# Rows gathered under the last strips, late rows added by extra gathers and accumulating scatters

## The reference

```python
h = jnp.maximum(_layernorm(x, axis=-1), 0.0)
x = x + _L0_gnn_ref(h, ...)     # tanh(h, t) W1 W2 + adj @ (h B^T) - rowsum(adj) * (h B^T)
h = jnp.maximum(_layernorm(x, axis=-1), 0.0)
x = x + _L1_gnn_ref(h, adj, ...)
# inside the second layer
feats = (X @ W).reshape(-1, H, D)
scores = jax.nn.leaky_relu(a_self.T[:, :, None] + a_neigh.T[:, None, :], negative_slope=0.2)
scores = scores + (-10000000000.0 * (1.0 - A))[None, :, :]
attn = jax.nn.softmax(scores, axis=-1)
out = relu(einsum('hij,jhd->ihd', attn, feats) + bias)
```

## Time and profile before

| | us |
|---|---|
| median of 3 runs | 891.37 (890.23 to 891.55) |
| the profiled execution | 890.93 |
| its span on the core | 889.1 |

### The profile page before, as it was taken

How to read it: one execution, slowest core, us unless ns; L and a number is a source line. 1 busy time by engine, 2 the same in 40 slices (tenths; PEclk the granted TensorE clock), 3 DMA queues, 4 the chain that set the end, 5 groups by cost and what they waited for, 6 DMA issues and landing times.

```text
span 889.1 us, 13351 instructions
## 1 busy us (share of the span) xinstructions
PE 765.8 (86%) x5222; PEld 275.1 (31%) x5222; DVE 728.0 (82%) x958; ACT 130.0 (15%) x212; POOL 173.9 (20%) x160
## 2 busy tenths in 40 slices
PE   3898999999999999999999999999999999940000
PEld 1323343333333333434343434333333333320000
DVE  5889889999898989898989898989989898943111
ACT  2424011111102020202020202011111102020000
POOL 1000303030201102030303030303020110217775
PEclk9999999999999999999999999999999999975555
DMA  9796898989898989898989989898989898501221
GB/s 372 280 429 255 342 389 327 393 330 389 336 387 364 382 342 386 332 391 335 386 337 383 371 348 392 328 392 328 392 328 392 359 384 352 221 17 40 52 58 43
DMA packets 37261, 281.48 MB, mean 317 GB/s; under 512 B 14336, under 2 KB 18560, under 8 KB 20736
## 3 DMA queue, kind: packets, MB, share of 16 engines
q1 hardware_dynamic: 24704, 275.02, 76.8%
q0 software_dynamic: 4096, 4.20, 2.0%
q10 hardware_dynamic: 8448, 2.10, 1.0%
HBM read 277.10 MB, written 4.19 MB: 316 GB/s over the span
## 4 chain that ended last, share of the span: by engine, by line
PE 83%; POOL 7%; SPq 4%; issue 3%; DMA 1%; DVE 1%; ACT 1%; POOLq 0%; ACTq 0%; DVEq 0%
PE acc L719 48%; PE row_sums L727 25%; POOL gathered L359 7%; SPq L256 4%; PE ps_hid L734 2%; PE ps_feat L776 1%; PE ps_xb L755 1%; PE ps_acc L748 1%; PE ps_turn L762 1%; DMA ring<-in_adj_t 1%; PE ps_acc L753 1%; PE ps_acc L751 1%; PE ps_turn L769 1%; POOL cand L350 0%; DMA gathered<-feats_dram,best 0%
## 5 line engine op out<-in xcount | busy, mean ns | idle before, releaser
L719 PE MATMUL acc<-ring,x_pb 128*64 128x512 f32 x2048 | 448.3, 594 | 0.0
L727 PE MATMUL row_sums<-ring,ones_cols 128*32 128x512 f32 x2048 | 234.3, 602 | 18.6 <-DMA ring<-in_adj_t 18.6
L505 DVE TENSOR_TENSOR max_lo<-max_lo,ring 128x2048 f32<-128x2048 f32 x96 | 219.7, 2288 | 37.5 <-DMA ring<-in_adj_t 36.7
L719 PEld LDWEIGHTS acc<-ring,x_pb 128*64 128x64 f32 x2048 | 143.8, 137 | 282.7 <-issue 280.9
L506 DVE TENSOR_TENSOR max_hi<-max_hi,ring 128x2048 f32<-128x2048 f32 x96 | 219.7, 2288 | 0.0
L350 POOL DMA_INDIRECT cand<-in_adj,cls_row x64 | 77.1, 1205 | 650.5 <-DVE cls_row L535 635.8
L727 PEld LDWEIGHTS row_sums<-ring,ones_cols 128*32 128x32 f32 x2048 | 61.6, 111 | 164.0 <-issue 159.2
L359 POOL DMA_INDIRECT gathered<-feats_dram,best x64 | 63.3, 989 | 19.5 <-issue 19.5
L643 DVE TENSOR_TENSOR gathered<-gathered,bias_row 128x512 f32<-128x512 f32 x8 | 5.6, 695 | 68.1 <-DMA gathered<-feats_dram,best 68.1
L427 ACT COPY feats<-ps_feat 128x320 f32 (+1 forms) x16 | 6.8, 426 | 216.4 <-PE ps_feat L776 216.4
L512 DVE TENSOR_TENSOR max_lo<-max_lo,max_hi 128x2048 f32<-128x2048 f32 x16 | 36.7, 2293 | 2.0
(11 more groups left out here) (95 smaller groups left out, 415.6 us busy)
## 6 DMA issues: line engine op xcount, KB each, us to landing
ring<-in_adj_t SPq DMA_DIRECT2D x128, 2048.0 KB, 9.3
x_tq<-in_x SPq DMA_DIRECT2D x1, 2048.0 KB, 31.0
feats_dram<-feats ACTq DMA_DIRECT2D x16, 128.0 KB, 2.6
out<-gathered SPq DMA_DIRECT2D x8, 256.0 KB, 2.2
x_pb<-in_x SPq DMA_DIRECT2D x1, 1536.0 KB, 7.8
cand<-in_adj,cls_row POOLq DMA_INDIRECT x64
gathered<-feats_dram,best POOLq DMA_INDIRECT x64, 2.4
x_pb<-in_x SPq DMA_DIRECT2D x1, 512.0 KB, 4.6
```

Source lines behind the costliest of these rows:

```text
L505: dve.tensor_tensor(max_lo[:, :], max_lo[:, :], lo, ALU.max).then_inc(lo_done, 1)
L719: last = pe.matmul(acc[0][at:at + D, :], x_pb[:, c * CB + b, :], slot(c)[:, b * W:(b + 1) * W], start=(c == 0 and b < 2), stop=(c == NC - ...
L727: last = pe.matmul(row_sums[at:at + QUAD, :], ones_cols[:, :], slot(c)[:, b * W:(b + 1) * W], start=(c == 0 and b < 4), stop=(c == NC - 1 ...
```

## The change

GpSimd keeps a DRAM table `agg_dram` in place of `feats_dram`: it holds relu(feats + bias). In the round of a strip GpSimd waits for ScalarE's copy of the features, adds the bias and takes the maximum with 0 in two instructions, issues the store from its own queue and waits until it has landed (`store_agg`). ScalarE's store is gone. Before the strips, the rows of strips 11 to 15 of the table are set to zero by five stores.

The 64 gathers are split into windows. Where the rows of `known` strips are in the table, tiles of strips s0 to s1 are gathered: 4, 16, 16, 16 and 8 tiles in the rounds 11 to 15, and 4 tiles at the end. A tile whose best row is not yet in the table reads zeros for it. VectorE lists up to 8 such late rows in each partition by their keys (`max` gives the 8 largest); GpSimd gathers those rows again in 8 indirect gathers at the end, and adds them to the output by 8 accumulating indirect scatters, four before and four after the gathers of the last two tiles. Partitions with fewer late rows spend the other slots on rows of the last strip, which is stored after all scatters. More than 8 late rows in a partition clear `good`, and so lead to the general path.

The last strip's table rows are computed by VectorE from PSUM (`agg_last`) and stored by SP. On VectorE the classes of the last strip are searched before its residual. x1 is added to the gathered rows in three instructions (52, 8 and 4 tiles) in place of sixteen; the output goes out in four stores, the first of which only fills the last strip. At the start, the first chunk is issued between the two pieces of x, x_tq comes after chunk 7, and the 17 weight loads move from SP's queue to GpSimd's.

```diff
+WINDOWS = ((11, 0, 1), (12, 1, 5), (13, 5, 9), (14, 9, 13), (15, 13, 15))
+EARLY = 13 * TB
+LATE = 15 * TB
...
+            load_x(0, 0, 2 * CB)
+            sp.dma_start(slot(0), adj_t[0]).then_inc(chunk_in[0], 16)
+            load_x(1, 2 * CB, NB)
+            for n in range(1, RING):
+                sp.dma_start(slot(n), adj_t[n]).then_inc(chunk_in[n], 16)
...
             for c in range(RING, NC):
                 load(0, c)
+            sp.dma_start(x_tq[:, :, :].rearrange("q (s k) d -> q s (k d)", k=TB), x_by_q).then_inc(x_tq_in, 16)
...
+            sp.dma_start(out_by_q[:, S - 1, :], x_pb[:, 0:TB, :].rearrange("q k d -> q (k d)")).then_inc(stored, 16)
+
+            sp.wait_ge(got[len(WINDOWS) - 1], 16 * (LATE - EARLY))
+            sp.wait_ge(agg_last_ready, 2)
+            sp.dma_start(agg_by_q[:, S - 1, :], agg_last[:, :, :].rearrange("q k d -> q (k d)")).then_inc(agg_last_stored, 16)
...
+            store(0, 0, EARLY)
+            store(1, EARLY, LATE)
+            sp.wait_ge(late_out, 16 * SLOTS)
+            store(2, LATE, NB)
...
+            for z in range(WINDOWS[0][0], S):
+                pool.dma_start(agg_by_q[:, z, :], agg[:, :]).then_inc(zero_stored, 16)
...
+            def store_agg(s):
+
+                pool.wait_ge(feat_done, s + 1)
+                a = feats_v[:, bass.ds(s * TB, TB), 0:D]
+                pool.tensor_tensor(agg[:, :].rearrange("q (k d) -> q k d", d=D), a,
+                                   bias_row[:, :].unsqueeze(1).to_broadcast([P, TB, D]), ALU.add).then_inc(agg_chain, 1)
+                pool.wait_ge(agg_chain, s * 2 + 1)
+                pool.sem_inc(pool_past, 1)
+                pool.tensor_scalar(agg[:, :], agg[:, :], 0.0, None, ALU.max).then_inc(agg_chain, 1)
+                pool.wait_ge(agg_chain, s * 2 + 2)
+                pool.dma_start(agg_by_q[:, bass.ds(s, 1), :].rearrange("q a f -> q (a f)"), agg[:, :]).then_inc(agg_stored, 16)
+                pool.wait_ge(agg_stored, s * 16 + 16)
...
+            for w, (known, s0, s1) in enumerate(WINDOWS):
+                add_b2(known)
+                if w:
+                    pool.wait_ge(got[w - 1], 16 * TB * (WINDOWS[w - 1][2] - WINDOWS[w - 1][1]))
+                store_agg(known - 1)
+                pool.wait_ge(best_done, s1)
+                if known < S - 1:
+                    gather(w, s0 * TB, s0 * TB + TB)
+                    fetch_candidates(known)
+                    gather(w, s0 * TB + TB, s1 * TB)
+                else:
+                    gather(w, s0 * TB, s1 * TB)
+                    fetch_candidates(known)
+
+
+            pool.wait_ge(agg_last_stored, 16)
+            pool.wait_ge(late_ready, 2)
+            for k in range(SLOTS):
+                pool.indirect_dma_start(
+                    out=late_agg[:, k, :], out_offset=None, in_=agg_dram,
+                    in_offset=bass.IndirectOffsetOnAxis(ap=late_from[:, k:k + 1], axis=0),
+                ).then_inc(late_in, 16)
+            pool.wait_ge(best_done, S)
+            gather(len(WINDOWS), LATE, LATE + 2)
+            pool.wait_ge(late_in, 16 * SLOTS)
+            pool.wait_ge(stored, 16 * 3)
+
+            def scatter(k):
+                pool.indirect_dma_start(
+                    out=out, out_offset=bass.IndirectOffsetOnAxis(ap=late_row[:, k:k + 1], axis=0),
+                    in_=late_agg[:, k, :], in_offset=None, compute_op=ALU.add,
+                ).then_inc(late_out, 16)
+
+            for k in range(TB):
+                scatter(k)
+            gather(len(WINDOWS), LATE + 2, NB)
+
+            pool.wait_ge(late_out, 16 * TB)
+            for k in range(TB, SLOTS):
+                scatter(k)
...
+            for known, s0, s1 in WINDOWS:
+                dve.tensor_scalar(is_late[:, s0 * TB:s1 * TB], best[:, s0 * TB:s1 * TB], float(known * W), None, ALU.is_ge)\
+                    .then_inc(late_chain, 1)
+            dve.tensor_tensor(late_key[:, :], best[:, 0:LATE], late_span[:, :], ALU.add).then_inc(late_chain, 1)
...
+            for w in range(len(WINDOWS) - 1):
+                dve.wait_ge(got[w], 16 * TB * (WINDOWS[w][2] - WINDOWS[w][1]))
+            add_x1(0, EARLY)
             search_candidates(S - 1)
+            dve.wait_ge(got[len(WINDOWS) - 1], 16 * (LATE - EARLY))
+            add_x1(EARLY, LATE)
```

More of the change, by code:

```diff
@@ L61, in sem @@
             return ctx.enter_context(nc.semaphore(name))
-        feats_dram = nc.dram_tensor("feats_dram", (N, D), F32, kind="Internal").ap()
+        agg_dram = nc.dram_tensor("agg_dram", (N, D), F32, kind="Internal").ap()
         neigh_dram = nc.dram_tensor("neigh_dram", (HEADS, N), F32, kind="Internal").ap()
@@ L185, in build @@
         best_done = sem("best_done")
-        got = [sem(f"got{g}") for g in range(QG)]
+        got = [sem(f"got{w}") for w in range(len(WINDOWS) + 1)]
+        late_chain = sem("late_chain")
+        late_ready = sem("late_ready")
+        late_in = sem("late_in")
+        late_out = sem("late_out")
         end_chain = sem("end_chain")
@@ L241, in _, with load_x @@
         def _(sp):
-            for k, (b0, b1_) in enumerate(((0, 2 * CB), (2 * CB, NB))):
+            def load_x(k, b0, b1_):
                 sp.dma_start(x_pb[:, b0:b1_, :], x_by_p[:, b0:b1_, :]).then_inc(x_in[k], 16)
[L244 to L261, removed]
+            load_x(0, 0, 2 * CB)
[3 more added lines that the diff above has]
+                sp.dma_start(slot(n), adj_t[n]).then_inc(chunk_in[n], 16)
             def load(s, c):
@@ L353, in _, with gather @@
                     ).then_inc(cand_in, 16)
[L354 to L358, removed]
-                pool.indirect_dma_start(
-                    out=gathered[:, t, :], out_offset=None, in_=feats_dram,
-                    in_offset=bass.IndirectOffsetOnAxis(ap=best[:, t:t + 1], axis=0),
-                ).then_inc(got[t // OG], 16)
+            def gather(w, t0, t1):
+                for t in range(t0, t1):
+                    pool.indirect_dma_start(
+                        out=gathered[:, t, :], out_offset=None, in_=agg_dram,
+                        in_offset=bass.IndirectOffsetOnAxis(ap=best[:, t:t + 1], axis=0),
+                    ).then_inc(got[w], 16)
@@ new lines, in round_ @@
+            def round_(s):
+                add_b2(s)
+                store_agg(s - 1)
+                fetch_candidates(s)
+            add_b2(0)
+            fetch_candidates(0)
+            n0 = WINDOWS[0][0]
+            with pool.Fori(1, n0) as s:
+                round_(s)
+            for w, (known, s0, s1) in enumerate(WINDOWS):
[11 more added lines that the diff above has]
+                    fetch_candidates(known)
@@ new lines, in _ @@
+            dve.scalar_tensor_tensor(late_at[:, :], late_s[:, :], -float(P), late_base[:, :], ALU.mult, ALU.add)\
+                .then_inc(late_chain, 1)
+            dve.wait_ge(late_chain, n + 7)
+            dve.tensor_tensor(late_row[:, :], late_at[:, :], late_k[:, :], ALU.subtract).then_inc(late_ready, 1)
+            dve.wait_ge(feat_ready, S)
+            dve.tensor_tensor(agg_last[:, :, :], ps_feat[:, :, 0:D], bias_row[:, :].unsqueeze(1).to_broadcast([P, TB, D]),
+                              ALU.add).then_inc(agg_last_ready, 1)
@@ new lines, in _, with add_x1 @@
+            dve.wait_ge(agg_last_ready, 1)
+            dve.tensor_scalar(agg_last[:, :, :], agg_last[:, :, :], 0.0, None, ALU.max).then_inc(agg_last_ready, 1)
+            def add_x1(t0, t1):
+                dve.tensor_tensor(gathered[:, t0:t1, :], gathered[:, t0:t1, :], x_tq[:, t0:t1, :], ALU.add)\
+                    .then_inc(out_done, 1)
+            for w in range(len(WINDOWS) - 1):
+                dve.wait_ge(got[w], 16 * TB * (WINDOWS[w][2] - WINDOWS[w][1]))
+            add_x1(0, EARLY)
@@ L637, in _ @@
             dve.tensor_scalar(flag[:, :], ps_hid[0:1, 0:1], P - 0.5, None, ALU.is_lt).then_inc(flag_done, 1)
[L640 to L649, removed]
+            dve.wait_ge(got[len(WINDOWS)], 16 * (NB - LATE))
+            add_x1(LATE, NB)
             dve.wait_ge(flag_done, 1)
```

97 lines of the change are left out of this document (76 added, 21 removed).

## The result

The changed kernel takes 858.74 us (median of 4 runs, 855.85 to 861.41) where the kernel before takes 891.46: a ratio of 0.9635, with a 95% interval of 0.9603 to 0.9668. It is faster, by 32.7 and not by the 61.7 of the forecast, and outside the range of 820 to 844. The profiled execution took 859.08, its span is 857.4.

The account below looks back on a forecast made before the run. TensorE was taken to bound the strips, GpSimd's issuing of gathers the end, and late chunk loads the start. Gains of 53.2 (end) and 8.5 (start), zero for the loop, sum to 61.7: forecast 829.5 us, range 820 to 844.

Parts of the forecast that it names:

- The loop: In the strips: GpSimd's added instructions, store with wait, and sixteen gathers in windows 12 to 14 were taken as zero cost.
- Twelve follow it: 758.9 + 15.5 + 1.95 = 776.4, with 2.0 to spare: In a strip's round: twelve gathers behind the candidate fetch take 15.5 and end before the features at 778.4.
- The end: Behind the last strip: fewer gathers, with late gathers and accumulating scatters added, end the span at 835.9, a gain of 53.2.
- The start: Before the first strip ends: earlier first chunk and no hole before chunk 4 give 9.4 on TensorE, 8.5 taken.
- All of this costs nothing: At the start: moving x_tq, chunk 8, weights and zeros is free while chunks 4 to 9 stay ahead of TensorE.
- rival 1: At the end: scatters at 2.87, landings of 4.8 and a direct store at 2.87 add 17, giving 846; chance 0.2.
- rival 2: At the start: no gain, as x_tq, zeros and weights only move the hole to another chunk: 838; chance 0.1.
- rival 3: In the loop: VectorE becomes the bound and TensorE stands 2.3 a strip, 34 in all: 863; chance 0.04.
- rival 4: At the end: the accumulating scatter runs row by row, 12.8 each, making the kernel slower at 921; chance 0.02.
- rival 5: In the late-row list: a partition with over 8 late rows leads to the general path, over 20 ms; chance 0.01.
- a strip above 47.5: In the loop: a sign that the forecast is wrong, where strips of 46.9 would show it right.
- the lower end of 821: Bottom of the 0.63-chance interval up to 837: scatter as a gather, direct store at 0.6, short maximum, all 9.4 of the start.

Follow-up runs that it names:

- experiment 1: Changed kernel with VectorE's folds on 512 columns in place of 2048 and the final test's limits opened: 844.33 us in one run.
- experiment 3: Changed kernel without the 12 gathers behind the candidate fetch in windows 13 and 14: 841.96 us in one run.
- experiment 4: Changed kernel with windows of 12, 12, 16, 12 and 8 tiles in place of 4, 16, 16, 16 and 8: 845.49 us, ratio 0.9484.
- experiment 6: experiment 5 with x1 added to the 52 early tiles in one instruction again, not 13 pieces: 839.40 us, ratio 0.944.
- experiment 5: experiment 4 with each round's landing wait moved behind store_agg's two computing instructions and the 52-tile x1 add cut into 13 pieces: 836.01 us, ratio 0.9381.
- experiment 10: Changed kernel with scatters that write and don't add, so late rows lose their x1: 853.38 us in one run.
- experiment 9: experiment 5 with GpSimd waiting for chunk 1 before it issues the weights and, behind them, the stores of zeros: 833.34 us, ratio 0.9357.
- experiment 8: experiment 5 with chunk 2 issued once chunk 0 has landed and chunk 3 once the second piece of x has: 836.36 us.

## Why the prediction was wrong

The sign was right, and so was the account of what bounds the kernel; the size was half. In spans, the forecast was 889.1 - 61.7 = 827.4, and 857.4 was measured: 30.0 too much, which lie so.

- **The loop, 9.0.** The step that failed is "Twelve follow it: 758.9 + 15.5 + 1.95 = 776.4, with 2.0 to spare". It priced a gather in the loop at the 1.295 of the end, where VectorE runs no folds. Measured 2.2 from one to the next beside folds, 26.9 for the lot. To this come two waits that the loop's count lacked or had short: 4.50 for the landing of the lot, and 6.35 for the landing of GpSimd's store in place of 3.4. The sign was in the earlier trace rows: a candidate fetch of 2.87 beside a fold, which I used only as an upper bound for operations without a row. It was in the 1.295 too, which I had put down to "a longer one now and then". Of the 64 gathers before, six took 1.34 to 1.46, and each lay beside an add of two inputs and ended 0.82 after it:

```profile
821.16 1.38 POOL L359 DMA_INDIRECT gathered<-feats_dram,best  x1 [0.30 <-issue]
```

```profile
821.03 0.69 DVE L643 TENSOR_TENSOR gathered<-gathered,bias_row 128x512 f32<-128x512 f32 x1 [8.50 <-DMA gathered<-feats_dram,best]
```

  Experiments 1, 3, 4 and 6 show the hold and its price, experiment 5 that of the waits.
- **The end, 17.3** (70.9 for 53.6). GpSimd issues its first gather of the last window 12.7 after the last turn of the maxima and not 4.3, from the same overrun: 8.4 (in experiment 5 it was 4.1). One gather beside the 52-tile add: 3.0. Eight scatters 1.86 apart and not 1.4: 3.7, the accumulating shown by experiment 10. A wait for the landing of the late gathers: 1.9. The end behind the last scatter, 8.4 and not 6.9: 1.5. Together 18.5, of which the plain calls at 1.26 give about 1 back.
- **The start, 3.7.** The hole before chunk 4 is gone, as said. But chunk 1 landed 3 late, since "All of this costs nothing" held the weights and zeros for free on GpSimd's queue; experiment 9 shows the cost, and that the step was right without it. Another 1.2 went at row sums of strip 1 (5.34 for 32, before 4.19 in the same place; 3.64 with the narrow folds of experiment 1). Why stays open.

The rule of the Trainium skill that I weighed (SBUF — State Buffer, Who interferes with whom: a VectorE instruction with two inputs in SBUF and a GpSimd one that reads SBUF exclude each other) was the right one, applied to the wrong instructions and in the wrong direction. I asked what GpSimd's adds do to VectorE; that was small, as said: from 73 to 600 us VectorE is busy 492.34 / 527 x 46.86 = 43.8 a strip, before 43.2. What counts is what VectorE's folds do to GpSimd's indirect calls, and there the trace agrees: in experiment 6 the call ends 0.84 after the add, as the others end about 0.82 after a fold.

Of the rivals, 1 had the scatter right in kind (1.56 for a call, between its ends) and its sum of 846 still missed. Rivals 2, 3, 4 and 5 did not happen: the start gave 5 to 6, no strip but the last ones stretched, a scatter lands in 3.2, and the general path did not run. The forecast's own sign of being wrong, "a strip above 47.5", did come: 50.0 from 687.45 to 737.45. One sum of the forecast does not hold by its own terms: the lower end of 821 is explained by a scatter as a gather, a direct store at 0.6, a short maximum and all 9.4 of the start, which together are under 4 and give about 826.

## What to carry to other kernels

Before work is moved under a busy stage, price it by a row from inside that stage: the same call cost 1.25 at the end and 2.2 under the folds. An engine with 39 us of idle time a strip did not have room for 16 calls in three rounds running, because it stands between two due times; a lot that overruns its round is paid by every engine behind it. Spreading the same 52 gathers evenly was worth 13 us, about 2 of them in the start, which the order does not touch, and moving a wait behind work that does not need it, with the adds cut in pieces, another 9.5. Small loads put on another queue are not free where large loads are on the path.

## What the runs showed of the hardware

- An indirect gather on GpSimd takes 0.95 alone. It is held until the end of a VectorE instruction with two inputs in SBUF that was already running, and in the changed kernel ends 0.80 to 0.90 after it; in experiment 6 it took 4.17 beside one add of 3.60. A call that begins just before the fold is not held (657.92, 0.94, beside the fold of 658.04). Direct stores from the same queue, 14 of 15 under folds, took 0.64 each.
- A direct store of 128 KB from GpSimd's queue lands after 6.7 (median) in the loop and after 2.1 at the least; ScalarE's store of the same size landed after 2.6 with the DMA engines as busy (share 0.90, here 0.89). Why was not tried.
- An accumulating scatter of 128 rows costs 1.56 a call where a plain one costs 0.98.
- TensorE's second chunk began with row sums of 3.47 in the changed kernel (granted clock 0.50, which is 1.2 GHz, from 22.5 to 25 us) and of 1.92 in experiment 5 (granted clock 1.00, 2.4 GHz), after idle times of 2.70 and 1.64. This alone moves the start by 1.5 between profiles of kernels with the same start. Five more profiles with 2.98 to 3.60 had idle times of 2.16 to 2.82; but experiment 8 had 1.92 after 3.22. What decides it stays open.
